# Where ScalarE rounds the next weight chunk in the MLP loop of a four-layer float32 kernel

## The reference

```python
def _gemma_mlp(x, gate_w, up_w, down_w):
    g = jnp.einsum('bsh,hi->bsi', x, gate_w)
    u = jnp.einsum('bsh,hi->bsi', x, up_w)
    return jnp.einsum('bsi,ih->bsh', jax.nn.gelu(g, approximate=True) * u, down_w)
...
att = jnp.einsum('bthd,btgd->bthg', q, k) / np.sqrt(HD).astype(np.float32)
att = jax.nn.softmax(att, axis=-1)
out = jnp.einsum('bthg,btgd->bthd', att, v).reshape(b, t, D)
...
gate = jax.nn.softmax(h2 @ Wg + bg, axis=-1)
combined = jnp.einsum('btd,edf,bte->btf', h2, We, gate)
```

## Time and profile before

| what | value |
|---|---|
| runs of the kernel | 1729.36, 1732.60, 1734.81 us |
| the profiled execution | 1735.44 us |
| its span, first to last instruction | 1733.7 us |
| mean granted TensorE clock, as a share of full speed | 0.917 |
| busy: PE, DVE, POOL, ACT | 87%, 66%, 38%, 32% of the span |

### The profile page before, as it was taken

How to read it: one execution, slowest core, us unless ns; L and a number is a source line. 1 busy time by engine, 2 the same in 40 slices (tenths; PEclk the granted TensorE clock), 3 DMA queues, 4 the chain that set the end, 5 groups by cost and what they waited for, 6 DMA issues and landing times.

```text
span 1733.7 us, 19836 instructions
## 1 busy us (share of the span) xinstructions
PE 1502.1 (87%) x7420; PEld 1271.0 (73%) x7420; DVE 1148.6 (66%) x1977; ACT 560.7 (32%) x786; POOL 652.6 (38%) x268
## 2 busy tenths in 40 slices
PE   5997899999889978999998898987899889976628
PEld 4896799997668967899976676766677667755416
DVE  7597655546875976544568523378748975896984
ACT  2202243442232022344323343533452345332001
POOL 3320133322322201333222344366656654754552
PEclk9897989998998979899989899999999999996758
DMA  5300011111112100111111132221221212100001
GB/s 178 111 25 13 25 37 50 49 38 37 37 55 67 36 1 25 49 42 46 37 37 45 55 115 76 89 70 58 74 79 53 93 55 80 67 25 25 25 16 45
DMA packets 22592, 92.72 MB, mean 53 GB/s; under 512 B 3408, under 2 KB 3808, under 8 KB 22368
## 3 DMA queue, kind: packets, MB, share of 16 engines
q1 hardware_dynamic: 21168, 88.18, 15.4%
q10 hardware_dynamic: 1328, 3.27, 0.5%
HBM read 89.35 MB, written 2.10 MB: 53 GB/s over the span
## 4 chain that ended last, share of the span: by engine, by line
PE 34%; DVE 17%; POOL 7%; issue 7%; ACT 4%; DVEq 0%; POOLq 0%; ACTq 0%
PE bank L291 11%; PE bank L295 10%; PE bank L294 10%; POOL w_lo L413 4%; DVE G L313 3%; ACT w_hi L1030 2%; DVE bank L1532 2%; POOL VW L313 2%; DVE acc L1556 2%; DVE F L1556 1%; PE bank L759 1%; DVE acc L1688 1%; DVE hid_hi L1485 1%; PE bank L558 0%; PE bank L574 0%
## 5 line engine op out<-in xcount | busy, mean ns | idle before, releaser
L413 POOL TENSOR_TENSOR w_lo<-raw,w_hi 128x1536 fp32r<-128x1536 f32 x48 | 169.3, 3526 | 291.3 <-ACT w_hi L1030 265.6
L291 PE MATMUL bank<-x_hi,w_hi 128*128 128x512 f32 x448 | 188.3, 420 | 63.0 <-POOL w_lo L413 38.3
L401 POOL CAST w_hi<-raw 128x1024 fp32r<-128x1024 f32 (+2 forms) x42 | 49.8, 1185 | 481.4 <-issue 447.1
L1409 DVE TENSOR_TENSOR hid_lo<-F,hid_hi 128x1024 fp32r<-128x1024 f32 x64 | 82.3, 1288 | 166.6 <-ACT hid_hi L980 166.4
L294 PE MATMUL bank<-x_lo,w_hi 128*128 128x512 f32 x448 | 182.2, 407 | 0.0
L295 PE MATMUL bank<-x_hi,w_lo 128*128 128x512 f32 x448 | 181.6, 405 | 0.0
L291 PEld LDWEIGHTS bank<-x_hi,w_hi 128*128 128x128 f32 x448 | 89.2, 199 | 93.8 <-POOL w_lo L413 48.8
L404 POOL TENSOR_TENSOR w_lo<-raw,w_hi 128x1024 fp32r<-128x1024 f32 (+2 forms) x51 | 129.2, 2534 | 65.6 <-ACT w_hi L903 62.2
L975 ACT ACTIVATE F<-bank,vecs 128x512 f32<-128x512 f32 x128 | 81.2, 686 | 199.3 <-PE bank L295 199.3
L291 PE MATMUL bank<-hid_hi,w_hi 128*128 128x512 f32 x320 | 127.9, 400 | 11.4 <-DVE hid_lo L1487 6.5
L294 PE MATMUL bank<-hid_lo,w_hi 128*128 128x512 f32 x320 | 126.1, 394 | 0.0
(11 more groups left out here) (331 smaller groups left out, 4072.0 us busy)
## 6 DMA issues: line engine op xcount, KB each, us to landing
raw<-in_skill SPq DMA_DIRECT2D x32, 768.0 KB, 4.2
raw<-in_l SPq DMA_DIRECT2D x40, 512.0 KB, 3.5
raw<-in_shared SPq DMA_DIRECT2D x16, 768.0 KB, 4.2
K<-in_l3e SPq DMA_DIRECT2D x16, 512.0 KB, 3.6
raw<-in_l0c SPq DMA_DIRECT2D x12, 512.0 KB, 3.6
raw<-in_qkv SPq DMA_DIRECT2D x8, 768.0 KB, 4.2
xT<-in_x ACTq DMA_DIRECT2D x4, 512.0 KB, 7.1
VW<-in_l1w SPq DMA_DIRECT2D x1, 2048.0 KB, 8.9
```

The lines of the kernel that those rows point to most:

```text
L291: i = nc.tensor.matmul(out, sh, mh, start=first, stop=False)
L413: nc.gpsimd.tensor_tensor(w_lo[n % W3_SLOTS][:], raw[n % 2][:], w_hi[n % W3_SLOTS][:].bitcast(F32), ALU.subtract).then_inc(w_ready.sem, 1)
L1409: v.tensor_tensor(hid_lo[u][:, hs, :], F[u][:], hid_hi[u][:, hs, :].bitcast(F32), ALU.subtract).then_inc(e1_hid.sem, 1)
```

## The change

In even slots ACT's `dense_hi(n)` moves from behind the rounding of the MLP tile to ahead of the wait for the gate half. Nothing is added or removed, and no other engine's order changes.

```diff
@@ -1115,6 +1115,8 @@
                         attention3_before(q, i, x, y)
                     if 0 <= p < BATCH:
                         finish3_before(p, i, x, y)
+                    if i % 2 == 0 and 2 <= n < CHUNKS3 * BATCH:
+                        dense_hi(n)
                     if b < BATCH:
                         act.wait_ge(*g3_ready(0, g + 1))
                         if g >= 2:
@@ -1128,8 +1130,6 @@
                         elif g == 0:
                             act.wait_ge(*f2_down(PAIRS - 1, 15))
                         nc.scalar.activation(hid_hi[0][:, g % HID3, :], PB[g % 2][1][:], ACT.Copy).then_inc(g3_hi.sem, 1)
-                    if i % 2 == 0 and 2 <= n < CHUNKS3 * BATCH:
-                        dense_hi(n)
                     if 0 <= q < BATCH:
                         attention3_after(q, i)
                     if 0 <= p < BATCH:
```

## The result

| what | before | after |
|---|---|---|
| median of 18 runs each, us | 1733.04 | 1739.30 |
| lowest and highest, us | 1727.41, 1737.14 | 1734.19, 1747.61 |
| the profiled execution, us (span) | 1735.44 (1733.7) | 1739.12 (1737.3) |
| granted TensorE clock over the span | 0.917 | 0.908 |

The ratio is 1.004, with a 95% interval of 1.0028 to 1.0052: 6.3 us slower on the medians. I predicted 1733.0 us (+0.4) and a range of 1714 to 1742. The time is inside the range, though 1.3 us above the 1728 to 1738 of the forecast itself, and the interval's lower end lies just under the 0.3% that I wanted to tell from no change, its upper end over it. So "within 0.3%" was close, but the change is slower, not neutral.

The account below looks back on a forecast made before the run. PE stalls on w_lo first, then from slot 10 of batch 1 DVE, mutually excluded with POOL, was taken as the bound. -17.7 + 8.5 - 1.7 + 3.1 + 5.5 + 2.7 = +0.4 us gave 1733.0 us, range 1714 to 1742.

Parts of the forecast that it names:

- Steps 1 to 4: Layer 3 through batch 1's attention values (slots 22 to 27): -17.7, +8.5, -1.7 and +3.1 us in turn.
- step 1: Batch 0 to slot 6 of batch 1: PE's stalls waiting for w_lo go, -17.7 us.
- the tie of 0.1 us: Even DVE-bound slots: POOL's sweep behind w_lo is issued 0.1 us ahead of DVE's product, making the slot 6.8 us.
- step 2: Scores of batch 1, slots 10 to 17: DVE's products wait for w_lo and sweeps, some +8.5 us.
- step 3: Softmax of batch 1: subtraction -2.6, multiplication +3.0, product of slot 21 -2.1; together -1.7 us.
- Step 5: Batch 2: expert gate 3.4 us later, slots 13 to 17 -0.3, subtraction, multiplication, later products, values; together +5.5 us.
- later products: Batch 2, DVE's products after the softmax multiplication: -0.9 us.
- Step 6: Batch 3 repeats batch 2 without the values term, as no chunk is left to round: +2.7 us.
- A: DVE's product wins the tie in even slots, so batch 1's pairs cost as before: 1722 us; chance 0.25.
- B: POOL and DVE settle so that exclusion costs as little as before: -17.7 to -25, about 1711 us; chance 0.15.
- C: Slots 13 to 23 of batches 2 and 3: expert sums don't cover the sweeps; 1741 to 1747 us; chance 0.20.
- D: The rounding waits for the load or d3_step and ACT blocks the gelu; chance 2 in 100.

Follow-up runs that it names:

- the kernel with the late w_lo: The change, with POOL's w_lo from slot 10 of batch 1 on also waiting for the hid_hi of its own slot; 1711.22 us.
- the first kernel above: The kernel before, with the rounding moved early only in batch 0 and slots 0 to 8 of batch 1; 1714.29 us.
- the even-sweep kernel: The change, with POOL's sweep waiting for DVE's product of its own slot in even slots only; 1718.84 us.

## Why the prediction was right or wrong

**Steps 1 to 4 held,** each within 0.2 us, and so did the mechanism that they stand on. PE's stalls went whole (step 1). POOL won the tie of 0.1 us in the even slots (step 2); the price of a pair, 6.8 + 6.5 us, is the measured one. That the price is the tie's is shown by the kernel in which the product wins by construction: 11.16 us in slots 14 to 17. The exact +8.5 has some luck in it: slots 10 and 11 cost 1.55 us and not 2.2, and the three pairs 6.96 us and not 7.0 - 0.6. The 0.6 us of DVE's wait for POOL was taken off twice, since the 10.91 us of a pair, counted from start to start, already held it. In step 3 the slot of the subtraction became 2.62 us shorter and that of the multiplication 2.97 longer (-2.6 and +3.0). The Trainium skill, page "SBUF — State Buffer", section "Who interferes with whom", has issue order decide who blocks; the rows of after agree at 0.09 and 0.11 us between the two, closer than any row of before.

**Step 5 was 2.0 us short** (+5.5 against +7.5). The gate's sum was right (3.36 us against 3.4), but 0.7 of it is the gelu behind rounding and table load, for which I had no term; the kernel with the late w_lo shows this part alone. The subtraction and the multiplication were right too; slots 13 to 17 gave -0.06 for -0.3. Slots 20 to 23 gave +0.07 instead of "later products -0.9", and the values +2.05 instead of +2.8. Another 1.6 us, between the gated products of slots 10 and 11, is TensorE's clock. The windows view of after and then of before, the slices in which the clock was low (us, busy time and count by engine, then the granted clock):

```profile
1275.00:1280.00 5.00, 5.00 (x36) 4.88 (x35) 4.34 (x3) 1.92 (x3) 5.00 (x3) 0.80 0.48 175
1280.00:1285.00 5.00, 5.00 (x16) 4.29 (x17) 0.00 (x0) 2.04 (x3) 2.10 (x1) 0.51 0.01 5
```

```profile
1290.00:1295.00 5.00, 5.00 (x19) 4.04 (x19) 0.00 (x0) 2.14 (x3) 5.00 (x3) 0.66 0.45 157
```

PE is busy in all of them, and was busy in the slices ahead; the clock falls to the lower level, 1.2 GHz, in both, by these shares for about 3.4 us in before and 6.9 us in after. It isn't part of the change's mechanism: the same slot of batch 3 shows 0.0 us, the kernel with only the gate slots early doesn't show it, and the first kernel above, whose order is that of before in this slot, loses the same 1.6 us there. Other traces have such a loss elsewhere (in the even-sweep kernel 1.6 us at the start of layer 3). Why it lasts longer in one execution stays open. The clock over the whole span was lower in all 18 runs of the change (0.902 to 0.910) than in the runs of before beside the experiments (0.914 to 0.920). No run here separates what that costs in the other slots, but it is not the main part of the loss: the even-sweep kernel, 20 us faster than the change, ran at 0.906 to 0.913.

**Step 6 failed: +2.7 against +6.9.** I wrote that batch 3 "repeats this", and carried over the -0.9 of the later products. In batch 2 the one large wait that goes is that of slot 23's product (2.98 us before, 1.86 after, 1.1 us of the slot), behind the w_lo of slot 22 and the sweep queued with it. Batch 3 has no such w_lo: the last chunk is rounded in slot 20. Timeline, POOL and DVE, slots 20 to 23 of batch 3, before and then after:

```profile
1531.89 1.22 DVE L313 TENSOR_TENSOR G<-F,VW 128x1024 f32<-128x1024 f32 x1
1534.16 3.50 POOL L413 TENSOR_TENSOR w_lo<-raw,w_hi 128x1536 fp32r<-128x1536 f32 x1 [13.44 <-ACT w_hi L1030]
1537.23 1.52 DVE L313 TENSOR_TENSOR G<-F,VW 128x1024 f32<-128x1024 f32 x1
...
1542.84 1.60 DVE L313 TENSOR_TENSOR G<-F,VW 128x1024 f32<-128x1024 f32 x1
```

```profile
1527.17 4.21 DVE L1581 TENSOR_TENSOR F<-F,mk 128x1024 f32<-128x1024 f32 x1
...
1531.46 5.66 POOL L313 TENSOR_TENSOR VW<-F,VW 128x1024 f32<-128x1024 f32 x2 [1.16 <-DVE F L1581]
1532.87 2.01 DVE L313 TENSOR_TENSOR G<-F,VW 128x1024 f32<-128x1024 f32 x1
...
1544.02 2.38 POOL L313 TENSOR_TENSOR VW<-F,VW 128x1024 f32<-128x1024 f32 x1 [6.89 <-DVE acc L1556]
1544.45 3.03 DVE L313 TENSOR_TENSOR G<-F,VW 128x1024 f32<-128x1024 f32 x1
```

With w_lo out of the way in slot 19, both first sweeps run behind the multiplication, ahead of the products. From slot 20 to slot 23 this costs 2.1 us, and 0.6 more to the end. Batch 2 has the same cost, 1.2 us from slot 20 to slot 23, which slot 23 only just makes up for: so the term had left a cost out in step 5 already. The kernel with only slot 20 early shows the same (+2.4 and +0.7), and holding the sweeps of the even slots back leaves +0.35 to slot 23. Against the term of -0.9 that is 3.6 of the 4.2 us; the gate (3.75 instead of 3.4) and slots 13 to 17 (0.0 instead of -0.3) make up the rest.

**The rivals.** A (the product wins the tie) didn't happen, but its price was right once forced, in two pairs of three. B (the exclusion costs as little as before) is false in the change, where every product of slots 10 to 17 takes 3.1 to 3.4 us. C (slower, because the expert sums don't cover the sweeps) has the right sign and the wrong place: slots 13 to 17 of batches 2 and 3 moved by -0.06 and 0.0 us, covered as I worked out; of the slots that C named only 20 to 23 of batch 3 lost time, some 2 us and not three pairs' worth. D is excluded by the trace of after: ACT stood idle ahead of none of the 46 roundings. What I missed as a case of its own was the sum of small terms in batches 2 and 3, each of the sign "DVE waits more". The chance for slower, 0.21, was too low for a sum of +0.4 with four places where a sweep had just been moved ahead of a product.

## What to carry to other kernels

Where two engines exclude each other at a port, an earlier start of one is a cost to the other: find what each freed operation of POOL will be issued ahead of on DVE, at each place that repeats and at the places where the pattern ends. The early rounding was worth 18 us where PE was the bound, and the rest of it had to be held back: by place (1712 us), or better by a wait of POOL's own operations for DVE's short one (1702 us). A term worked out for one batch may be carried to the next only after looking whether the operation that made it is still there.

## What the runs showed of the hardware that I hadn't expected

A wait added to an engine can shorten a kernel: POOL held back behind DVE's product saves 24 us against the change, and 5 us (1711.94 to 1706.81) in the kernel whose roundings already avoid the collisions, nearly all of it in a stage without any rounding. Being blocked shows as busy time of the blocked instruction, not as a wait: DVE's share rose from 66% to 68% by waiting, and the waits view of slots 13 to 19 of batch 1 has no wait of DVE for POOL. A lead of 0.05 us is enough, in either direction. In after, in slot 0 of batch 2, the sweep is issued at 1207.79 and the product at 1207.84 takes 3.42 us; in the kernel with the late w_lo a product issued at 1284.25 takes 1.23 us, and the w_lo issued 0.04 us behind it, at 1284.29, takes 4.47. And the reductions beside them are not held up: the sum at 1141.91 takes 1.20 us in the middle of a w_lo.
